# GpSimd's gathers wait, four by four, for marks that TensorE sets in its own program

## The chip, the cores and the metric

The kernel runs on one core of a Trainium2 chip. The metric is the device time of one execution in microseconds (us), the median of several runs. Engines are named as in the profile: PE is TensorE (PEld its weight loads), DVE is VectorE, ACT is ScalarE, POOL is GpSimd, SP is SyncE, whose DMA queue is SPq.

## The reference, cut to what matters

Thirty-two images of 64x64x3 go through a tokenizer of four spectral layers (a truncated Fourier transform, a product with weights for each mode, the transform back, a 1x1 convolution and a gelu). Its 64 tokens are put ahead of 128 text tokens, and the 192 tokens of each image go through four mixers: a recurrent one, a mixture of experts, an attention, and a product-key memory. The memory is the part that the change touches: each token and head picks 16 rows of a table of 32,768 rows, for the keys and the values alike, and sums them with softmax weights:

```python
kv_scores, indices = _pk(x, Wq_pk, pk_keys)           # 8 heads, 16 rows of 4096 each
ind = indices + offsets[None, None, :, None]
k = jnp.einsum('bnhk,bnhkd->bnhd', kv_scores, keys_table[ind])
v = jnp.einsum('bnhk,bnhkd->bnhd', kv_scores, values_table[ind])
sim = jnp.einsum('bihd,bjhd->bhij', q, k)             # causal softmax, then times v, then @ Wo
```

## The kernel before

The work is in pairs of images for the mixers (16 pairs, numbered 0 to 15) and in groups of four for the tokenizer (8 groups). A pair has 384 tokens, three tiles of 128. It needs 3 x 8 = 24 **units**, one per tile and head. A unit is 16 gathers: gather k fetches, for each of 128 tokens, the row of `in_table` (key and value side by side, 128 floats) that `IDX[:, tile, head, k]` names, into one of four slots of `GATH` (`RING = 4`, slot u % 4). So there are 384 gathers a pair and 6,144 in all, every one an indirect DMA that POOL issues at L670, and POOL does nothing else after its first memsets.

POOL's loop (`pool_gather`) walks the units in order. Ahead of units 0, 8 and 16 of a pair it waits until VectorE has written the indices of the tile (`kept_idx`), and ahead of each unit until VectorE has emptied the slot that unit u - 4 had (`gather_free`). Each unit then is used twice. ScalarE (`a_consume`, L886) waits for the 16 transfers and multiplies each with its weight, and VectorE (`v_consume`, L893) sums the 16 into `KV` and gives the slot back.

All other engines run a program whose order is fixed when it is built. A **round** works on three things side by side: the mixers of pair i + 1, up to the choice of its 16 rows a head; the gathered rows of pair i (chain "rows"), which ScalarE and VectorE take up; and the end of pair i - 1 (chain "back"); in the rounds that have it, also two layers of the next tokenizer group. `weave` lays chains beside each other in windows. Each chain has steps with costs in `STEPS`, a step comes up at the share of its chain's cost that lies ahead of it, and the step with the smallest share is next, on every engine in the same manner. A round has two large windows. In the first, the chain of rows is a step "hold" of cost 1 and then units 0 to 10 (`U1 = 11`); in the second it is units 11 to 23. So unit u of the first window stands at share (1 + u)/12. The first two rounds have their own lists (`first_rounds`): pair 0 has units 0 to 7 beside the first two tokenizer layers of group 1 ("alone"), then 8 to 15 and 16 to 23 in the two windows of "beside", beside the other two layers and the mixers of pair 1.

Each engine takes its instructions in order. Where ScalarE stands at a unit whose rows have not landed, all of its later work waits as well, and with it what TensorE needs from it. TensorE itself never touches the gathered rows; it first meets them as `KV`, in `t_back`.

`fence(e)` is one semaphore increment of the engine itself. It makes a semaphore instruction of its own, which carries a wait that stands ahead of it.

The gathers are issued in these lines of `pool_gather`:

```python
for u in range(NT3 * H):
    r = u % RING
    if u % H == 0: e.wait_ge(*event("kept_idx", i, u // H + 1))
    e.wait_ge(*event("gather_free", i, u + 1 - RING))
    fence(e)
    for k in range(TOPK):
        e.indirect_dma_start(GATH[:, r, k, :], None, table, bass.IndirectOffsetOnAxis(IDX[:, u // H, u % H, k:k + 1], 0)).then_inc(gath[r], 16)
```

Of the kernel before, what the change touches and what calls it, by code (L numbers as in the profile page):

```python
# [36 lines left out]
ROWQ = POS // 512  # L37
# [5 lines left out]
F_T = ROWQ + CHUNKS  # L43
# [37 lines left out]
NT3 = TOK // 128  # L81
E, FF, CAP = 8, 256, 960
H, TOPK, NK = 8, 16, 64
# [10 lines left out]
EPS = 1e-5  # L94
FMAX = float(np.finfo(np.float32).max)
RING = 4


FRONT = [("xT", 0, 1), ("rnn", 1, 2), ("rnn_back", 2, 1),
# [37 lines left out]
def total(plan, bank):  # L137
# [9 lines left out]
TOP_STEPS = 11  # L147

STEPS = {"coords": [2.2] * (GB * ROWQ), "forward0": [1.7] * F_T, "mix0": [5.3] * CHUNKS, "inverse0": [2.8] * CHUNKS + [2.2] * ROWQ,
         "tokens": [3.5] * (GB * ROWQ),  # L150
         "rnn": [4, 3, 2.5, 2.5, 1.2, 1.2, 1.2, 1.2], "moe": [2, 2.5, 2.5, 2.5, 3, 3, 3] + [4.6] * E + [6],
         "att": [2, 2.5, 2.5, 2.5, 1.5] + [3] * 5 + [3.3] * 6 + [5, 5], "pk": [2, 2.5, 2.5, 2.5, 1.5, 2.5, 2.5, 2.7, 2.7, 2.7],
         "top": [3, 3, 3, 3, 4, 4, 4, 4, 4, 4, 2] * NT3,
         "back": [3.5] * 3 + [2.6] * 4 + [2.2] * 3 + [7] * 7 + [4], "keep_x": [2], "rows": [1] * NT3 * H, "ahead": [1] * H, "hold": [1]}
STEPS.update({s + "1": STEPS[s + "0"] for s in ("forward", "mix", "inverse")})
BACK_IN = 3
U1 = 11
# [35 lines left out]
def whole(*sections):  # L193
    return [(s, 0, len(STEPS[s])) for s in sections]
# [5 lines left out]
def a_round(begin=(), layers=True, end=(), front=True, rows=True, back=True):  # L200


    tokenizer = [[*begin, *LAYER_0], ["forward1", "mix1", "inverse1", *end]] if layers else [[], []]
    turned = [("back", 0, BACK_IN)] if back else []
    return ([] if front else [[turned]]) + [
            [turned + whole("rnn", "moe", "att", "pk") if front else [], whole(*tokenizer[0]), whole("hold") + [("rows", 0, U1)] if rows else []],
            [whole("top") if front else [], [("back", BACK_IN, len(STEPS["back"]))] if back else [], whole(*tokenizer[1]),
             [("rows", U1, NT3 * H)] if rows else []],
            [whole("keep_x")]]


def first_rounds():


    alone = [[whole("rnn", "moe", "att", "pk")],
             [[("top", 0, TOP_STEPS)], whole("coords") + [("forward0", 0, ROWQ)]],
             [[("top", TOP_STEPS, len(STEPS["top"]))], [("forward0", ROWQ, F_T)] + whole(*LAYER_0[1:], *LAYER_1), whole("hold", "ahead")],
             [whole("keep_x")]]
    beside = [[whole("rnn", "moe", "att", "pk"), whole(*LAYER_0), [("rows", H, 2 * H)]],
              [whole("top"), whole(*LAYER_1, "tokens"), [("rows", 2 * H, NT3 * H)]],  # L220
              [whole("keep_x")]]
    return alone, beside

# [4 lines left out]
def early_fusion(nc, xT, fc0, sw, cwb, fc1, fc2, f1, f2, g3, g4, txt, wrnn, brnn, gw, w1, w2, b2, wq, wk, wv, wot, wpk, keysT, wq5, wo5,  # L228
# [3 lines left out]
    with ctx:  # L232
# [55 lines left out]
        empt = {(k, b): sem(f"{k}_out{b}") for k in PLANS for b in range(4)}  # L288
        PER = {"x_in": 80, "normed": 4, "shifted": 1, "exped": 1, "one_hot": 1, "h_kept": 1, "maxed": 24, "masked": 12,
               "rden": 2, "shift_top": NT3, "exp_top": NT3, "kept_idx": NT3, "kept_wt": NT3, "kept_x": 1,  # L290
               "gather_free": NT3 * H, "weighted": 1, "maxed5": 12, "scaled5": 6, "out_sb": 1, "stored": 16, "multiplied": NT3 * H}
        S = {n: sem(n) for n in PER}
        gath = [sem(f"gathered{r}") for r in range(RING)]
        tokenizer_in, const_in, zeroed = sem("tokenizer_weights_in"), sem("mixer_weights_in"), sem("buffers_zeroed"); mask_rows = sem("mask_rows_set")
# [6 lines left out]
        def fence(e):  # L301

            e.sem_inc(passed[str(e.engine).split(".")[-1]], 1)


        def event(name, it, k):

            return S[name], (it + 1) * PER[name] + k
# [352 lines left out]
        def pool_gather(e, i):  # L661
            for u in range(NT3 * H):
                r = u % RING

                if u % H == 0: e.wait_ge(*event("kept_idx", i, u // H + 1))

                e.wait_ge(*event("gather_free", i, u + 1 - RING))
                fence(e)
                for k in range(TOPK):
                    e.indirect_dma_start(GATH[:, r, k, :], None, table, bass.IndirectOffsetOnAxis(IDX[:, u // H, u % H, k:k + 1], 0)).then_inc(gath[r], 16)  # L670


# [416 lines left out]
        def q_slots(h, bank):  # L1089
# [2 lines left out]
            if h < 7: return [(QT[:, :, :, QSLOT[h], :], src)]  # L1092
            return [(QT[:, :, 2, 7, :], src[:, :, 0, :]), (QT[:, :, 0:2, 7, :], src[:, :, 1:3, :])]

        def t_turn(e, j, name, k):
            e.wait_ge(*event("normed", j, k))
            e.wait_ge(*free("front", j, name))
            fence(e)
            for t in range(NT3):
                m = e.transpose(PB[0][0:64, 128 * t:128 * t + 128], N[:, t, :], ID[:, :])  # L1100
            m.then_inc(full["front", 0], 1)
# [139 lines left out]
        def t_pk(e, j):  # L1241
            yield 4
            t_turn(e, j, "pkT", 4)
            yield 5
            e.wait_ge(*emptied("front", j, "pkT"))
            for n in range(4):
                yield 5 + n // 2
                name = ("qpkA", "qpkB")[n % 2]
                e.wait_ge(*free("front", j, name, n // 2))
                fence(e)  # L1250
                e.matmul(PB[2 + n % 2][:, 0:TOK], WPK[:, 128 * n:128 * n + 128], NT4[:, :], start=True, stop=True).then_inc(full["front", 2 + n % 2], 1)
            yield 7
            e.wait_ge(*emptied("front", j, "qpkA", 1)); e.wait_ge(*emptied("front", j, "qpkB", 1))
            for t in range(NT3):
                yield 7 + t
                for p in range(2):
                    name = ("simA", "simB")[p]
                    e.wait_ge(*free("front", j, name, t))
                    fence(e)
                    for hh in range(2):  # L1260
                        m = e.matmul(PB[2 + p][:, 256 * hh:256 * hh + 256], QPK[:, 2 * p + hh, 128 * t:128 * t + 128], KB[:, 2 * p + hh, :], start=True, stop=True)
                    m.then_inc(full["front", 2 + p], 1)
# [115 lines left out]
        def TENSOR(e, k, i, j, g, l):  # L1378
            return {"coords": lambda: t_coords(e, g), "forward0": lambda: t_forward(e, g, l, 0), "forward1": lambda: t_forward(e, g, l + 1, 0),
                    "mix0": lambda: t_mix(e, g, l), "mix1": lambda: t_mix(e, g, l + 1), "inverse0": lambda: t_inverse(e, g, l, 0), "inverse1": lambda: t_inverse(e, g, l + 1, 0),  # L1380
                    "tokens": lambda: t_tokens(e, g), "rnn": lambda: t_rnn(e, j), "moe": lambda: t_moe(e, j), "att": lambda: t_att(e, j),
                    "pk": lambda: t_pk(e, j), "back": lambda: t_back(e, k)}

        def SCALAR(e, k, i, j, g, l):
            return {"coords": lambda: a_coords(e, g), "forward0": lambda: a_forward(e, g, l, 0), "forward1": lambda: a_forward(e, g, l + 1, 0),
# [18 lines left out]
        @block.gpsimd  # L1404
        def _(e):
            def before(e):
                for t in (FW0, FW1, FW2, CONV, KB, ONES, RS, OHS, AREA4, SW, WO5):
                    e.memset(t[:], 1.0 if t is ONES else 0.0).then_inc(zeroed, 1)
            before(e)
            with e.Fori(0, PAIRS) as i:  # L1410
                pool_gather(e, i)

# [99 lines left out]
```

## Time and profile before

| what | us |
|---|---|
| median of 3 runs | 8628.49 |
| lowest and highest of them | 8618.34, 8636.04 |
| the profiled execution's own time | 8612.81 |
| its span in the trace | 8611.0 |
| POOL, first and last gather's start | 631.7, 8518.5 |
| POOL, sum of its gathers | 5933.5 |

The span is the part of the execution that the trace covers, 1.8 us less than the execution's own time. A busy time is the sum of an engine's instructions, without those that only wait, count or branch. For GpSimd a gather's busy time is the time in which it makes the descriptors, not the transfer. An idle time in brackets stands ahead of an instruction, with what ended it; "issue" there means that nothing the profile shows was waited for. L numbers are lines of the kernel before.

### The profile page before, as it was taken

How to read it: one execution, taken by the hardware profiler on the slowest of the kernel's cores; microseconds unless marked ns; L12 is line 12 of the kernel's file. 1: busy time of each engine (PE TensorE's matmuls, PEld its weight loads, DVE VectorE, ACT ScalarE, POOL GpSimd, SP SyncE). 2: the span in 40 equal slices, each digit the busy share in tenths (PEclk: the TensorE clock that was granted, in tenths of full speed). 3: DMA queues.
4: the chain of work that ended last, by engine and by line, in shares of the span. 5: the costliest groups of instructions: out<-in, count | busy, mean ns of one | idle time of the engine just before them, and what ended most of it. 6: DMA issues, size and time to landing. Idle time of an engine off the chain costs nothing.

```text
span 8611.0 us, 111801 instructions
## 1 busy us (share of the span) xinstructions
PE 6113.0 (71%) x30064; PEld 4613.3 (54%) x30064; DVE 4933.1 (57%) x16123; ACT 3291.5 (38%) x9885; POOL 5939.7 (69%) x6159
## 2 busy tenths in 40 slices
PE   6868979787877879787887879687887865242104
PEld 5547756666565646666565646566565643121103
DVE  1246484848575674847575674847566573736422
ACT  1213334444434344444443444344443443333222
POOL 0007667777777777777777777777777777777774
PEclk7766666666666666566656666566666665555555
DMA  1102222222222222222222222222222222121111
GB/s 30 17 7 68 52 52 59 60 59 60 63 60 61 60 57 61 60 60 60 63 60 60 60 58 61 58 62 60 63 60 58 59 58 53 51 54 51 53 53 32
DMA packets 660625, 471.63 MB, mean 55 GB/s; under 512 B 560624, under 2 KB 561008, under 8 KB 659632
## 3 DMA queue, kind: packets, MB, share of 16 engines
q0 software_dynamic: 196608, 403.05, 17.7%
q1 hardware_dynamic: 463344, 60.87, 4.5%
q8 instruction: 268, 4.39, 0.2%
q14 instruction: 405, 3.32, 0.1%
HBM read 461.32 MB, written 2.10 MB: 54 GB/s over the span
## 4 chain that ended last, share of the span: by engine, by line
POOL 60%; issue 20%; PE 13%; DVE 4%; SPq 1%; DVEq 1%; ACT 1%; DMA 1%; POOLq 0%; ACTq 0%
POOL GATH L670 60%; PE MM L457 3%; PE MM L472 1%; DVE KV L893 1%; PE PB L1205 1%; PE PB L1193 1%; PE MM L493 1%; PE MM L496 1%; PE MM L409 1%; PE TP L466 1%; PE PB L1141 1%; PE PB L1213 0%; PE PB L1172 0%; PE MM L432 0%; SPq L625 0%
## 5 line engine op out<-in xcount | busy, mean ns | idle before, releaser
L670 POOL DMA_INDIRECT GATH<-in_table,IDX x6144 | 5933.5, 966 | 2579.3 <-issue 2491.8
L886 ACT ACTIVATE GATH<-GATH,WT 128x128 f32<-128x128 f32 x6144 | 1883.3, 390 | 1961.1 <-DMA GATH<-in_table,IDX 1960.2
L893 DVE TENSOR_REDUCE KV<-GATH 128x128 f32<-128x2048 f32 x384 | 1392.8, 3627 | 1223.3 <-ACT GATH L886 1215.6
L457 PE MATMUL MM<-SPEC,SW 128*128 128x8 f32 (+1 forms) x8800 | 1153.5, 288 | 101.8 <-DMA SW<-in_sw 70.2
L457 PEld LDWEIGHTS MM<-SPEC,SW 128*128 128x128 f32 (+1 forms) x8800 | 1146.3, 248 | 139.4 <-issue 137.1
L566 DVE COPY TURN<-TP 80x512 f32<-80x512 f32 (+1 forms) x512 | 345.3, 684 | 451.1 <-PE TP L489 277.5
L1323 PE MATMUL PB<-AREA 128*64 128x64 f32 (+1 forms) x2304 | 317.5, 298 | 361.6 <-ACT AREA L1083 361.4
L409 PE MATMUL MM<-F,TURN 128*128 128x80 f32 x2048 | 367.2, 339 | 195.2 <-DVE TURN L566 191.3
L1323 PEld LDWEIGHTS PB<-AREA 128*64 128x64 f32 (+1 forms) x2304 | 255.3, 192 | 443.0 <-issue 395.0
L409 PEld LDWEIGHTS MM<-F,TURN 128*128 128x128 f32 x2048 | 337.8, 250 | 247.6 <-issue 186.8
L525 ACT ACTIVATE U<-MM 128x320 f32<-128x320 f32 (+1 forms) x416 | 218.7, 526 | 644.3 <-PE MM L409 390.9
L496 PEld LDWEIGHTS MM<-G,TURN 80*128 80x128 f32 x2048 | 315.0, 222 | 242.9 <-issue 125.2
L570 DVE COPY TURN<-TP 128x512 f32<-128x512 f32 (+1 forms) x320 | 216.9, 682 | 359.4 <-PE TP L466 212.2
L496 PE MATMUL MM<-G,TURN 80*128 80x128 f32 x2048 | 320.3, 307 | 69.0 <-DVE TURN L566 69.0
L493 PE MATMUL MM<-IMG,CONV 128*128 128x512 f32 x512 | 326.6, 725 | 29.0 <-ACT IMG L525 29.0
L472 PE MATMUL MM<-G,TURN 40*128 40x128 f32 x1280 | 300.4, 408 | 62.9 <-DVE TURN L570 62.7
L525 ACT ACTIVATE IMG<-MM,CONV 128x512 f32<-128x512 f32 x256 | 174.8, 684 | 434.8 <-PE MM L496 433.2
L472 PEld LDWEIGHTS MM<-G,TURN 40*128 40x128 f32 x1280 | 269.3, 304 | 111.1 <-issue 89.2
L1141 PE MATMUL PB<-NTR,W1E 104*128 104x384 f32 x512 | 279.6, 684 | 36.8 <-ACT AREA L984 36.8
L525 ACT ACTIVATE SPEC<-MM 128x160 f32<-128x160 f32 x320 | 95.1, 297 | 547.4 <-PE MM L457 308.0
L1205 PE MATMUL PB<-KT,AREA 64*128 64x192 f32 x768 | 260.2, 513 | 50.9 <-ACT AREA L1007 38.2
L869 DVE TENSOR_REDUCE PF<-SEARCH 128x16 f32<-128x800 f32 (+1 forms) x288 | 268.0, 931 | 30.7 <-issue 8.1
(214 smaller groups left out, 9843.0 us busy)
## 6 DMA issues: line engine op xcount, KB each, us to landing
GATH<-in_table,IDX POOLq DMA_INDIRECT x6144
SW<-in_sw SPq DMA_DIRECT2D x1280, 40.0 KB
CONV<-in_cwb SPq DMA_DIRECT2D x128, 4.0 KB
CONV<-in_cwb SPq DMA_DIRECT2D x128, 0.1 KB
U<-in_xT SPq DMA_DIRECT2D x16, 96.0 KB
out<-OUTB SPq DMA_DIRECT2D x16, 96.0 KB, 1.9
W1E<-in_w SPq DMA_DIRECT2D x1, 512.0 KB
W2E<-in_w SPq DMA_DIRECT2D x1, 512.0 KB
```

Source lines behind the costliest of these rows:

```text
L409: m = e.matmul(p[:, 80 * j:80 * j + 80], TURN[:, c % 2, 128 * j:128 * j + 128], F1[:, :], start=True, stop=True)
L457: m = e.matmul(pv[r, :, k, :], SW[r, half, k % HM, w:w + WID * beside], Sv[r, :, c * MODES + k, :], start=True, stop=True)
L472: m = e.matmul(p[:, 128 * a:128 * a + 128], TURN[0:40, i % 2, 128 * a:128 * a + 128], G3[:, :], start=True, stop=True)
L493: e.matmul(p[:, :], CONV[:, 0:128], IMG[:, q, 512 * c:512 * c + 512], start=True, stop=False, skip_group_check=True)
L496: m = e.matmul(p[:, 128 * j:128 * j + 128], TURN[0:80, (CHUNKS + c) % 2, 128 * j:128 * j + 128], G4[:, :], start=False, stop=True, skip_gr ...
L525: e.activation(dst, MM[n % 2][src] if not callable(src) else src(MM[n % 2]), func, **kw).then_inc(mm_out, 1)
L670: e.indirect_dma_start(GATH[:, r, k, :], None, table, bass.IndirectOffsetOnAxis(IDX[:, u // H, u % H, k:k + 1], 0)).then_inc(gath[r], 16)
L886: m = e.activation(GATH[:, r, k, :], GATH[:, r, k, :], ACT.Copy, scale=WT[:, u // H, u % H, k:k + 1])
L893: e.tensor_reduce(KV[:, u // H, :, u % H, :], GATH[:, u % RING, :, :].rearrange("p k (c d) -> p c d k", c=2), AX.X, ALU.add).then_inc(S["g ...
L1141: e.matmul(PB[2 + n % 2][:, 0:TOK], W1[:, 128 * n:128 * n + 128], NTR[:, :], start=True, stop=True).then_inc(full["front", 2 + n % 2], 1)
L1205: m = e.matmul(PB[2 + n % 2][:, SEQ * a:SEQ * a + SEQ], QT[:, b, r, 2 * c:2 * c + 2, :], KT[:, SEQ * b:SEQ * b + SEQ], start=True, stop=True)
L1323: m = e.matmul(o, PT[0:p0 + hi - lo, slot(c, p0), 64 * h:64 * h + 64], VW[0:p0 + hi - lo, t, h, :], start=(h == 0 and c == 0), stop=(h == ...
```

## The change

It adds a semaphore `paced` and a second counter of the work on it. TensorE gets a chain "pace" (and "pace_ahead" for the first third of pair 0) in the same windows as the chain of rows and with the same total cost: 96 steps a pair (`QUADS`), each of cost 4/16, each of which only adds 1 to the semaphore. Mark n of the first window thus stands at share (1 + n/4)/12 of it, where unit n/4 of the rows stands; marks 0 to 43 lie in the first window and 44 to 95 in the second. The chain stands in TensorE's list alone.

GpSimd gets, ahead of each four gathers (a **quad**, 96 a pair, quad n = 4u + k/4), a wait for the mark `LEAD = 8` quads behind it, and a fence: quad n may start once marks 0 to n - 8 of its pair are set. Quads 0 to 7 of a pair wait for the last marks of the pair before. The wait for the free slot and the one for the indices stay; the fence of each unit is gone, since the first quad's fence takes its place. GpSimd itself sets the first 96 counts, once, so that pair 0 starts with its first eight quads free.

```diff
--- before.py
+++ after.py
@@ -94,6 +94,9 @@
 EPS = 1e-5
 FMAX = float(np.finfo(np.float32).max)
 RING = 4
+QUAD = 4
+QUADS = 3 * 8 * 16 // QUAD
+LEAD = 8
 
 
 FRONT = [("xT", 0, 1), ("rnn", 1, 2), ("rnn_back", 2, 1),
@@ -151,7 +154,7 @@
          "rnn": [4, 3, 2.5, 2.5, 1.2, 1.2, 1.2, 1.2], "moe": [2, 2.5, 2.5, 2.5, 3, 3, 3] + [4.6] * E + [6],
          "att": [2, 2.5, 2.5, 2.5, 1.5] + [3] * 5 + [3.3] * 6 + [5, 5], "pk": [2, 2.5, 2.5, 2.5, 1.5, 2.5, 2.5, 2.7, 2.7, 2.7],
          "top": [3, 3, 3, 3, 4, 4, 4, 4, 4, 4, 2] * NT3,
-         "back": [3.5] * 3 + [2.6] * 4 + [2.2] * 3 + [7] * 7 + [4], "keep_x": [2], "rows": [1] * NT3 * H, "ahead": [1] * H, "hold": [1]}
+         "back": [3.5] * 3 + [2.6] * 4 + [2.2] * 3 + [7] * 7 + [4], "keep_x": [2], "rows": [1] * NT3 * H, "pace": [QUAD / 16] * QUADS, "pace_ahead": [QUAD / 16] * (QUADS // NT3), "ahead": [1] * H, "hold": [1]}
 STEPS.update({s + "1": STEPS[s + "0"] for s in ("forward", "mix", "inverse")})
 BACK_IN = 3
 U1 = 11
@@ -203,9 +206,9 @@
     tokenizer = [[*begin, *LAYER_0], ["forward1", "mix1", "inverse1", *end]] if layers else [[], []]
     turned = [("back", 0, BACK_IN)] if back else []
     return ([] if front else [[turned]]) + [
-            [turned + whole("rnn", "moe", "att", "pk") if front else [], whole(*tokenizer[0]), whole("hold") + [("rows", 0, U1)] if rows else []],
+            [turned + whole("rnn", "moe", "att", "pk") if front else [], whole(*tokenizer[0]), whole("hold") + [("rows", 0, U1)] if rows else [], whole("hold") + [("pace", 0, U1 * QUADS // 24)] if rows else []],
             [whole("top") if front else [], [("back", BACK_IN, len(STEPS["back"]))] if back else [], whole(*tokenizer[1]),
-             [("rows", U1, NT3 * H)] if rows else []],
+             [("rows", U1, NT3 * H)] if rows else [], [("pace", U1 * QUADS // 24, QUADS)] if rows else []],
             [whole("keep_x")]]
 
 
@@ -214,10 +217,10 @@
 
     alone = [[whole("rnn", "moe", "att", "pk")],
              [[("top", 0, TOP_STEPS)], whole("coords") + [("forward0", 0, ROWQ)]],
-             [[("top", TOP_STEPS, len(STEPS["top"]))], [("forward0", ROWQ, F_T)] + whole(*LAYER_0[1:], *LAYER_1), whole("hold", "ahead")],
+             [[("top", TOP_STEPS, len(STEPS["top"]))], [("forward0", ROWQ, F_T)] + whole(*LAYER_0[1:], *LAYER_1), whole("hold", "ahead"), whole("hold", "pace_ahead")],
              [whole("keep_x")]]
-    beside = [[whole("rnn", "moe", "att", "pk"), whole(*LAYER_0), [("rows", H, 2 * H)]],
-              [whole("top"), whole(*LAYER_1, "tokens"), [("rows", 2 * H, NT3 * H)]],
+    beside = [[whole("rnn", "moe", "att", "pk"), whole(*LAYER_0), [("rows", H, 2 * H)], [("pace", QUADS // 3, 2 * QUADS // 3)]],
+              [whole("top"), whole(*LAYER_1, "tokens"), [("rows", 2 * H, NT3 * H)], [("pace", 2 * QUADS // 3, QUADS)]],
               [whole("keep_x")]]
     return alone, beside
 
@@ -288,7 +291,7 @@
         empt = {(k, b): sem(f"{k}_out{b}") for k in PLANS for b in range(4)}
         PER = {"x_in": 80, "normed": 4, "shifted": 1, "exped": 1, "one_hot": 1, "h_kept": 1, "maxed": 24, "masked": 12,
                "rden": 2, "shift_top": NT3, "exp_top": NT3, "kept_idx": NT3, "kept_wt": NT3, "kept_x": 1,
-               "gather_free": NT3 * H, "weighted": 1, "maxed5": 12, "scaled5": 6, "out_sb": 1, "stored": 16, "multiplied": NT3 * H}
+               "gather_free": NT3 * H, "weighted": 1, "maxed5": 12, "scaled5": 6, "out_sb": 1, "stored": 16, "multiplied": NT3 * H, "paced": QUADS}
         S = {n: sem(n) for n in PER}
         gath = [sem(f"gathered{r}") for r in range(RING)]
         tokenizer_in, const_in, zeroed = sem("tokenizer_weights_in"), sem("mixer_weights_in"), sem("buffers_zeroed"); mask_rows = sem("mask_rows_set")
@@ -665,8 +668,10 @@
                 if u % H == 0: e.wait_ge(*event("kept_idx", i, u // H + 1))
 
                 e.wait_ge(*event("gather_free", i, u + 1 - RING))
-                fence(e)
                 for k in range(TOPK):
+                    if k % QUAD == 0:
+                        e.wait_ge(*event("paced", i, (TOPK * u + k) // QUAD + 1 - LEAD))
+                        fence(e)
                     e.indirect_dma_start(GATH[:, r, k, :], None, table, bass.IndirectOffsetOnAxis(IDX[:, u // H, u % H, k:k + 1], 0)).then_inc(gath[r], 16)
 
 
@@ -1092,6 +1097,11 @@
             if h < 7: return [(QT[:, :, :, QSLOT[h], :], src)]
             return [(QT[:, :, 2, 7, :], src[:, :, 0, :]), (QT[:, :, 0:2, 7, :], src[:, :, 1:3, :])]
 
+        def t_pace(e, i, lo, hi):
+            for n in range(lo, hi):
+                yield n
+                e.sem_inc(S["paced"], 1)
+
         def t_turn(e, j, name, k):
             e.wait_ge(*event("normed", j, k))
             e.wait_ge(*free("front", j, name))
@@ -1379,7 +1389,7 @@
             return {"coords": lambda: t_coords(e, g), "forward0": lambda: t_forward(e, g, l, 0), "forward1": lambda: t_forward(e, g, l + 1, 0),
                     "mix0": lambda: t_mix(e, g, l), "mix1": lambda: t_mix(e, g, l + 1), "inverse0": lambda: t_inverse(e, g, l, 0), "inverse1": lambda: t_inverse(e, g, l + 1, 0),
                     "tokens": lambda: t_tokens(e, g), "rnn": lambda: t_rnn(e, j), "moe": lambda: t_moe(e, j), "att": lambda: t_att(e, j),
-                    "pk": lambda: t_pk(e, j), "back": lambda: t_back(e, k)}
+                    "pk": lambda: t_pk(e, j), "pace": lambda: t_pace(e, i, QUADS // NT3 if isinstance(i, int) and i == 0 else 0, QUADS), "pace_ahead": lambda: t_pace(e, j, 0, QUADS // NT3), "back": lambda: t_back(e, k)}
 
         def SCALAR(e, k, i, j, g, l):
             return {"coords": lambda: a_coords(e, g), "forward0": lambda: a_forward(e, g, l, 0), "forward1": lambda: a_forward(e, g, l + 1, 0),
@@ -1407,6 +1417,7 @@
                 for t in (FW0, FW1, FW2, CONV, KB, ONES, RS, OHS, AREA4, SW, WO5):
                     e.memset(t[:], 1.0 if t is ONES else 0.0).then_inc(zeroed, 1)
             before(e)
+            e.sem_inc(S["paced"], PER["paced"])
             with e.Fori(0, PAIRS) as i:
                 pool_gather(e, i)
```

GpSimd's program changes as follows. These are the rows at the start of its loop over pairs, before, for units 0 and 1 (`kept_idx` and `gather_free` are the waits):

```order
L667 ISA [waits kept_idx]
L670 DMA GATH<-in_table,IDX 128x128 [waits gather_free]
L670 DMA GATH<-in_table,IDX 128x128 x15
L667 REGISTER_ALU
L670 DMA GATH<-in_table,IDX 128x128 [waits gather_free]
L670 DMA GATH<-in_table,IDX 128x128 x15
```

And the end of unit 0 and the start of unit 1 after the change:

```order
L675 DMA GATH<-in_table,IDX 128x128 [waits paced]
L675 DMA GATH<-in_table,IDX 128x128 x3
L673 REGISTER_ALU
L675 DMA GATH<-in_table,IDX 128x128 [waits paced]
L675 DMA GATH<-in_table,IDX 128x128 x3
L670 REGISTER_ALU
L673 REGISTER_ALU [waits gather_free]
L675 DMA GATH<-in_table,IDX 128x128 [waits paced]
```

Every fourth gather now has a register instruction and a wait ahead of it, where before only every sixteenth had. The gathers and their order are the same.

On TensorE no matrix instruction moves. These are the rows of the rounds' loop near the end of the first window of an odd pair, before:

```order
L493 MATMUL MM<-IMG,CONV 128x512
L494 REGISTER_ALU
L496 MATMUL MM<-G,TURN 128x128 x4
L489 MATMUL TP<-IDB,U 80x128 x4
L493 MATMUL MM<-IMG,CONV 128x512
```

And after:

```order
L496 MATMUL MM<-IMG,CONV 128x512
L497 REGISTER_ALU
L499 MATMUL MM<-G,TURN 128x128 x4
L492 MATMUL TP<-IDB,U 80x128 x4
L496 MATMUL MM<-IMG,CONV 128x512
```

The list leaves out instructions that only count, so the marks are not seen in it: mark 36 of the odd pairs is set between the third and the fourth row (L499 and L492 after, L496 and L489 before).

## Rows read from the trace of the kernel before

**Rows 1.** The page, part 1 and part 2: busy time and span in slices.

```profile
PE 6113.0 (71%) x30064; PEld 4613.3 (54%) x30064; DVE 4933.1 (57%) x16123; ACT 3291.5 (38%) x9885; POOL 5939.7 (69%) x6159
...
POOL 0007667777777777777777777777777777777774
```

**Rows 2.** The page, part 4: chain that ended last.

```profile
POOL 60%; issue 20%; PE 13%; DVE 4%; SPq 1%; DVEq 1%; ACT 1%; DMA 1%; POOLq 0%; ACTq 0%
```

**Rows 3.** The page, part 5: gathers, their weighting, their sum (mean ns after busy us).

```profile
L670 POOL DMA_INDIRECT GATH<-in_table,IDX x6144 | 5933.5, 966 | 2579.3 <-issue 2491.8
L886 ACT ACTIVATE GATH<-GATH,WT 128x128 f32<-128x128 f32 x6144 | 1883.3, 390 | 1961.1 <-DMA GATH<-in_table,IDX 1960.2
L893 DVE TENSOR_REDUCE KV<-GATH 128x128 f32<-128x2048 f32 x384 | 1392.8, 3627 | 1223.3 <-ACT GATH L886 1215.6
```

**Rows 4.** Line L670: ns least, middle, most; first and last start.

```profile
L670 POOL DMA_INDIRECT GATH<-in_table,IDX x6144: 938/944/2368, 631.7 to 8518.5; - x199
```

**Rows 5.** Waits, 3158 to 3645 us (pair 5): us in total, times, longest.

```profile
POOL GATH L670 <- issue: 117.0, 384, 0.3
ACT GATH L886 <- DMA GATH<-in_table,IDX: 65.9, 9, 12.0
```

**Rows 6.** Waits, 631 to 1175 us (pair 0).

```profile
POOL GATH L670 <- DVE KV L893: 55.4, 8, 19.8
```

**Rows 7.** Waits, 1175 to 1693 us (pair 1).

```profile
POOL GATH L670 <- DVE KV L893: 32.0, 11, 12.5
```

**Rows 8.** Line L893 around 1030 us, and in time order GpSimd's next gather.

```profile
L893 DVE TENSOR_REDUCE KV<-GATH x1: 3644/3644/3644, 1032.0 to 1032.0; 128x128 f32<-128x2048 f32 x1
...
1036.45 0.94 POOL L670 DMA_INDIRECT GATH<-in_table,IDX  x1 [19.80 <-DVE KV L893]
```

**Rows 9.** Time order, GpSimd: first gather of unit 11, pairs 1, 3, 5, 7, 11.

```profile
1419.35 1.35 POOL L670 DMA_INDIRECT GATH<-in_table,IDX  x1 [0.30 <-issue]
...
2404.09 1.46 POOL L670 DMA_INDIRECT GATH<-in_table,IDX  x1 [0.30 <-issue]
...
3378.03 0.94 POOL L670 DMA_INDIRECT GATH<-in_table,IDX  x1 [0.30 <-issue]
...
4352.94 0.95 POOL L670 DMA_INDIRECT GATH<-in_table,IDX  x1 [0.30 <-issue]
...
6304.46 1.03 POOL L670 DMA_INDIRECT GATH<-in_table,IDX  x1 [0.30 <-issue]
```

**Rows 10.** Time order, TensorE: what follows mark 36, same five pairs.

```profile
1455.97 0.85 PE L489 MATMUL TP<-IDB,U 128*80 128x128 f32 x3
...
2403.14 0.60 PE L489 MATMUL TP<-IDB,U 128*80 128x128 f32 x4
...
3385.07 0.85 PE L489 MATMUL TP<-IDB,U 128*80 128x128 f32 x3
...
4354.01 0.63 PE L489 MATMUL TP<-IDB,U 128*80 128x128 f32 x2
...
6306.90 0.63 PE L489 MATMUL TP<-IDB,U 128*80 128x128 f32 x2
```

**Rows 11.** Time order, GpSimd: two waits of pair 1.

```profile
1440.65 0.94 POOL L670 DMA_INDIRECT GATH<-in_table,IDX  x1 [1.02 <-DVE KV L893]
...
1465.63 0.94 POOL L670 DMA_INDIRECT GATH<-in_table,IDX  x1 [5.32 <-DVE KV L893]
```

**Rows 12.** Time order, around 1338 and 1368 us: unit 6 of pair 1, gathered and taken up.

```profile
1338.21 0.94 POOL L670 DMA_INDIRECT GATH<-in_table,IDX  x1 [0.30 <-issue]
...
1367.96 1.26 ACT L886 ACTIVATE GATH<-GATH,WT 128x128 f32<-128x128 f32 x4
```

**Rows 13.** Time order, 2980 to 2985 us: long gathers beside VectorE.

```profile
2981.59 0.99 DVE L863 TENSOR_TENSOR SEARCH<-IOTA,PF 128x800 f32<-128x800 f32 x1
...
2981.76 1.64 POOL L670 DMA_INDIRECT GATH<-in_table,IDX  x1 [0.30 <-issue]
...
2982.66 0.99 DVE L866 TENSOR_TENSOR SEARCH<-SEARCH 128x800 f32<-128x800 f32 x1
```

## The prediction

> **What bounds the kernel now.** I read the busy times first, and they mislead: TensorE is busy for 6113.0 us and GpSimd for 5939.7 us, and neither reaches 72% of the span [rows 1]. The chain that ended last decides: 60% of it lies on GpSimd and 20% is "issue" [rows 2]. The gathers explain both numbers. There are 6144 of them, and of the 2579.3 us of idle time ahead of them 2491.8 us are "issue" [rows 3]. In pair 5 all 384 gathers have such an idle time, 117.0 us in all and at most 0.3 us each [rows 5], so a gather costs 0.944 us (the middle one) and a gap of 0.305 us, a cadence of 1.25 us. From the first gather at 631.7 us to the last at 8518.5 us [rows 4] lie 7887 us; 6143 cadences are 7673 us. The rest is 134 us by which gathers are longer than 0.944 us (5933.5 less 6144 x 0.944) [rows 3] and waits for VectorE, 55.4 us in pair 0 and 32.0 us in pair 1 [rows 6, 7]. So GpSimd issues without a pause from pair 2 on, and all others wait for it: ScalarE's weighting stands idle for 1960.2 us until gathers land [rows 3]. Only pairs 0 and 1 are bound by the other engines. Whatever stops GpSimd lengthens the kernel, unless it replaces a stop that is there already.
>
> **What the change does to this.** It removes and speeds up nothing on GpSimd. It adds a condition: a gather may run at most two units (8 quads) ahead of TensorE's place, where the ring lets it run four units ahead of VectorE's sums. I laid the 1,536 marks into TensorE's own order of matrix instructions, read when the instruction behind each mark started, and compared that with the start of the quad that would wait for it. The terms follow from this and from the added instructions.
>
> **Pairs 0 and 1.** Here TensorE is behind the gathers: by that count about three quarters of the marks come after the start of their quad, up to 53 us in pair 0. As the other engines set the pace here, what counts is the last mark that binds. That is mark 36 of pair 1, needed by the first gather of unit 11. The gather started at 1419.35 us [rows 9], and TensorE passed the mark just before 1455.97 us [rows 10]. A stopped gather also needs time to start again: VectorE's sum that frees a slot ended at 1032.0 + 3.644 = 1035.64 us and the gather began at 1036.45 us, 0.8 us later [rows 8]. So the unit starts at 1456.8 us, 37.4 us later. Behind it the kernel before had two stops, 1.02 and 5.32 us, each with the normal 0.3 us in it [rows 11]; a later GpSimd does not meet them: 37.4 - 0.7 - 5.0 = **31.7 us**. Then the others are late too. The last gather of unit 6 of pair 1 started at 1338.21 us, so it ended at 1339.15 us, and ScalarE took the unit up at 1367.96 us, 28.8 us later [rows 12]. By my pass over the marks GpSimd is some 33 us late there, and ScalarE takes rows up 2 us after the last gather where it waits, so it begins 33 + 2 - 28.8 = **6 us** late, and the marks behind with it. Together 38 us. In plain words: the lead of the ring, four units against two, is what GpSimd lived on while the others caught up, and about two units' time (2 x 20 us) is lost once.
>
> **Pairs 2 to 12.** All is in step with GpSimd, so a delay of GpSimd moves the marks as well, and the margins of the trace hold. The tight place is again mark 36, near the end of the first window. In the even pairs it is set 4 us or more in time. In the odd ones, with 0.8 us for the restart: pair 3, 2403.14 + 0.8 against 2404.09, just in time; pair 5, 3385.07 + 0.8 - 3378.03 = 7.8 us late; pair 7, 4354.01 + 0.8 - 4352.94 = 1.9 us; pair 9 has the same margin as pair 7; pair 11, 6306.90 + 0.8 - 6304.46 = 3.2 us [rows 9, 10]. Sum **15 us**. Pairs 13 to 15 have no tokenizer beside them and are 7 us or more in time: 0.
>
> **TensorE's own marks.** No row shows what one costs. The nearest: ahead of a unit's first gather GpSimd runs two small instructions, ahead of units 8 and 16 three, and all hide in a gap of 0.3 us [rows 5], so one is at most 0.1 us. Forty-four marks lie ahead of the tight place: 0 to 4.4 us in each of the six odd pairs up to 11, 0 to 26 us. Most fall where TensorE waits or has matrix work queued; I take 1 us each, **6 us**. Elsewhere they cost nothing while TensorE idles, which is its cover.
>
> **GpSimd's own instructions.** The new boundaries carry one register instruction and one wait, just what unit starts carried, and those 24 of pair 5 show no longer gap than the other 360 [rows 5]: 0. Only ahead of units 0, 8 and 16 there is one more than any boundary had: 48 x 0 to 0.1 = 0 to 5 us; I take **0**, since the gap has held every smaller number. Behind the waiting instruction stand all later gathers, and behind these ScalarE's weighting, VectorE's sum and through them TensorE; that is why nothing of the stops is hidden in pairs 2 to 12. The head up to 631.7 us and the tail behind the last gather are not touched; the one count that GpSimd sets at the start falls in the head.
>
> The Trainium skill ("Advanced Engine Details and Errata", Miscellaneous Facts) gives 50 to 100 ns for a sequencer's reading of a semaphore. Taken as time added to each of the 1,536 new waits that would be 77 to 154 us, an estimate from that page, and the sum would be 136 to 213 us. The trace's unit starts speak against it.
>
> **Sum:** 31.7 + 6 + 15 + 6 + 0 = 59 us. The profiled execution took 8612.8 us, so its like would take 8672 us; the median of the runs is 15.7 us above it, so I forecast 8628.5 + 59 = **8687 us**. Its own range is 8655 (only 32 in pairs 0 and 1 and a few us after them) to 8725 (marks at their upper bound, 20 us more, and pairs as tight as pair 5 more often). A measurement of this kernel can tell 0.2%, 17 us, from no change.
>
> **Rivals.**
> *No change that can be measured.* GpSimd stops 87.4 us in pairs 0 and 1 already [rows 6, 7]; if the marks' stops only take their place, and the others, with fewer gathers in flight, catch up sooner, 0 to 17 us remain: 8629 to 8645 us. It also holds the case that the marks never bind. Against it: the margins of rows 9 and 10 are 37 us in pair 1, and only 5.7 us of stops come behind it to be replaced. Chance 0.12.
> *Each wait has a price.* If the quads' boundaries aren't covered as the unit starts are, 1,536 waits at 0.05 to 0.1 us (the upper bound above and half of it) add 77 to 154 us: 8764 to 8841 us. It decides as soon as a plain boundary's gap is above 0.31 us. Chance 0.10.
> *Late everywhere.* The margins of pairs 1 to 11 are small against what TensorE's marks and its clock can move. If mark 36 comes 6 us later in all of them, even pairs begin to stop as well: about 11 x 6 = 66 us more, 8753 us. Chance 0.10.
> *Faster.* VectorE's search for the top rows lengthens gathers: the one at 2981.76 us took 1.64 us, while L863 and L866 ran beside it [rows 13]; all such excess is 134 us. If the pacing moved gathers off this work, up to 134 us come back: 8687 - 134 = 8553 us. It decides where more than 76 of the 134 us go. Against it: GpSimd still issues without a pause, so gathers can't be moved off anything; what it stops is 1% of its time. Chance 0.05.
> The Trainium skill ("GPSIMD Engine Reference", Specifications) says that GpSimd shares its SBUF interfaces with VectorE and contends with instructions that have two SBUF inputs; by that rule only gathers that don't meet L863 and L866 gain, and the trace agrees with its 1.64 against 0.94 us.
>
> **How the numbers follow.** The forecast has 0.63, and the rivals in their order 0.12, 0.10, 0.10 and 0.05. A range from 8637 to 8790 us leaves out the faster case, half of the no-change case, two thirds of the priced waits and the outer edges of the forecast, and keeps the late marks: about 8 in 10. Faster by over 0.2%: 0.05; within: 0.12; slower: 0.83.
>
> **What would show it.** Right: gathers of pairs 0 and 1 idle for some 110 us in all with TensorE's marks as what ended it, the last gather of pair 1 about 38 us later, pairs 2, 4, 6 with no stop, odd pairs with one of 2 to 8 us near unit 11, plain gaps still 0.30 us. The steps fail if the gap at quad boundaries is longer, if even pairs stop, or if the start of pair 2 has not moved.

## The result and the profile after

The change makes the kernel slower: 8660.70 us median (8646.95 to 8668.83, 8 runs) against 8633.45 us (8618.34 to 8640.72, 8 runs), a ratio of 1.0033 with a 95% interval of 1.0024 to 1.0042, or 21 to 36 us. The profiled execution took 8646.95 us with a span of 8645.1 us, 34 us more than that of before.

The page of the changed kernel: busy times, GpSimd's slices, the chain that ended last, and the three groups that handle the gathered rows (busy us, mean ns; idle us ahead of them and what ended most of it). They answer to [rows 1 to 3].

```profile
PE 6084.4 (70%) x30064; PEld 4590.2 (53%) x30064; DVE 4934.1 (57%) x16123; ACT 3291.4 (38%) x9885; POOL 5960.8 (69%) x6159
...
POOL 0007667777777777777777777777777777777774
...
POOL 36%; PE 30%; issue 15%; DVE 10%; ACT 3%; DMA 2%; PEld 2%; DVEq 1%; SPq 1%; POOLq 1%; PEldq 0%; ACTq 0%
...
L675 POOL DMA_INDIRECT GATH<-in_table,IDX x6144 | 5954.6, 969 | 2592.8 <-issue 2448.4
L891 ACT ACTIVATE GATH<-GATH,WT 128x128 f32<-128x128 f32 x6144 | 1883.5, 390 | 2101.4 <-DMA GATH<-in_table,IDX 2100.6
L898 DVE TENSOR_REDUCE KV<-GATH 128x128 f32<-128x2048 f32 x384 | 1392.4, 3626 | 1272.5 <-ACT GATH L891 1266.4
```

The busy times are those of before within 0.5%. The chain that ended last looks different, since it now crosses over to TensorE in the stops, and even where GpSimd never stops it may be followed back through the marks; it names TensorE for 30% of the span although nothing of TensorE got slower. The idle time ahead of the gathers tells more. Idle beyond the plain gap of 0.305 us, which I call **stops** from here on, is 2592.8 - 625.8 (ahead of the first gather) - 6143 x 0.3048 = 94.6 us; for the kernel before the same sum is 2579.3 - 624.9 - 1872.4 = 82.0 us [rows 3]. The rest of the 34 us is not idle time: the gathers themselves took 5954.6 us, 21.1 us more than before.

Line L675, the least, middle and longest gather in ns, and the starts of the first and last:

```profile
L675 POOL DMA_INDIRECT GATH<-in_table,IDX x6144: 939/947/2363, 632.5 to 8553.3; - x199
```

Between these starts lie 7920.8 us, before 7886.9 us [rows 4]. The middle gather took 947 ns and not 944; the experiments bear on whether that is the change's doing.

Where the stops are: waits of GpSimd in pair 0 (632 to 1200 us), then of GpSimd and ScalarE in pair 1 (1200 to 1716 us), then GpSimd's longest idle time behind it (total us, times, longest). These answer to [rows 5 to 7].

```profile
POOL GATH L675 <- PEq L1103: 77.9, 33, 12.6
...
ACT GATH L891 <- DMA GATH<-in_table,IDX: 84.7, 8, 14.5
...
POOL GATH L675 <- PEq L1103: 27.8, 22, 15.7
...
POOL GATH L675 <- issue: 1600.5, 5250, 0.3
```

"PEq L1103" is TensorE's sequencer at the line of the marks. A wait that doesn't stop anything still counts its 0.3 us. Pairs 0 and 1 have all the stops; from pair 2 on the longest idle time is 0.3 us at the 5,250 gathers of that row, and the others, put down to marks (120) or sums (7), have 0.3 us each as well. The waits for VectorE's sums (55.4 and 32.0 us before [rows 6, 7]) are gone, TensorE's marks stand in their place, and ScalarE, which waited for landing rows at units 21 and 23 of pair 1 before (6.5 and 5.5 us), now waits at unit 6 and at each from 16 on: 84.7 us up to unit 22 and 11.1 us at unit 23.

In time order, ScalarE in pair 1 of the changed kernel, at units 6 and 16:

```profile
1365.92 1.28 ACT L891 ACTIVATE GATH<-GATH,WT 128x128 f32<-128x128 f32 x4 [1.03 <-DMA GATH<-in_table,IDX]
...
1572.76 2.45 ACT L891 ACTIVATE GATH<-GATH,WT 128x128 f32<-128x128 f32 x8 [13.40 <-DMA GATH<-in_table,IDX]
```

And at unit 16 in the kernel before (the row begins with the last of unit 15):

```profile
1560.87 2.44 ACT L886 ACTIVATE GATH<-GATH,WT 128x128 f32<-128x128 f32 x8
```

Unit 6 is taken up at 1365.92 us, which is 2 us sooner than before [rows 12], though its last gather came 25 us later (1363.4 against 1338.2). Unit 16 is taken up 11 us later, after ScalarE stood idle for 13.40 us. So in this execution ScalarE's own timetable up to unit 15 of pair 1 hardly changed; it ran out of gathered rows for good at unit 16 and not at unit 21. Pair 2 begins at 1716.3 us and not at 1693.8, and this 22.5 us stays to the end.

### The profile page after: what moved, and what is told of

The parts are those of the page before. It is cut to its first block, busy times and chain, and to the rows that moved or that the text cites. A ratio compares the mean times of both kernels' runs of the same rounds, so it can differ in the third digit from the quotient of the medians.

```text
span 8645.1 us, 116003 instructions
## 1 busy us (share of the span) xinstructions
PE 6084.4 (70%) x30064; PEld 4590.2 (53%) x30064; DVE 4934.1 (57%) x16123; ACT 3291.4 (38%) x9885; POOL 5960.8 (69%) x6159
## 4 chain that ended last, share of the span: by engine, by line
POOL 36%; PE 30%; issue 15%; DVE 10%; ACT 3%; DMA 2%; PEld 2%; DVEq 1%; SPq 1%; POOLq 1%; PEldq 0%; ACTq 0%
POOL GATH L675 36%; PE MM L460 5%; DVE KV L898 2%; PE PB L1151 2%; PE PB L1203 2%; PE PB L1215 2%; PE PB L1223 2%; PE PB L1182 2%; ACT GATH L891 2%; PE MM L475 2%; DMA GATH<-in_table,IDX 1%; PE MM L496 1%; PE MM L393 1%; PE MM L499 1%; PE MM L412 1%
## 5 line engine op out<-in xcount | busy, mean ns | idle before, releaser
L675 POOL DMA_INDIRECT GATH<-in_table,IDX x6144 | 5954.6, 969 | 2592.8 <-issue 2448.4
L499 PEld LDWEIGHTS MM<-G,TURN 80*128 80x128 f32 x2048 | 316.7, 223 | 234.0 <-issue 126.8
L499 PE MATMUL MM<-G,TURN 80*128 80x128 f32 x2048 | 321.6, 308 | 62.4 <-DVE TURN L569 62.3
L496 PE MATMUL MM<-IMG,CONV 128*128 128x512 f32 x512 | 324.7, 721 | 38.7 <-ACT IMG L528 38.7
```

What stands on the lines that cost most here:

```text
L496: e.matmul(p[:, :], CONV[:, 0:128], IMG[:, q, 512 * c:512 * c + 512], start=True, stop=False, skip_group_check=True)
L499: m = e.matmul(p[:, 128 * j:128 * j + 128], TURN[0:80, (CHUNKS + c) % 2, 128 * j:128 * j + 128], G4[:, :], start=False, stop=True, skip_gr ...
```

## The experiments

Each ratio compares a kernel with the kernel before on the same chip. The last three columns come from one profiled execution each. Stops are computed as above from the page's row. "First to last" is from the start of the first gather to the start of the last. One chip ran the change a second time, the waits that never bind and the two kernels with waits in a part of the pairs; another ran the two leads and the ring. Which one ran the first comparison, with the profiles of the first two rows, isn't known. So the three columns can also differ by the chip; the ratios can't.

| kernel | ratio, 95% interval | stops, us | gathers, us | first to last, us |
|---|---|---|---|---|
| before | 1 | 82.0 | 5933.5 | 7886.9 |
| the change | 1.0033, 1.0024 to 1.0042 | 94.6 | 5954.6 | 7920.8 |
| the change, second time | 1.0041, 1.0027 to 1.0054 | 120.3 | 5941.3 | 7933.1 |
| waits that never bind | 1.0005, 0.9996 to 1.0014 | 84.5 | 5945.4 | 7901.4 |
| waits in pairs 0, 1 | 1.0031, 1.0020 to 1.0041 | 114.9 | 5938.0 | 7924.4 |
| waits from pair 2 | 1.0009, 1.0000 to 1.0018 | 87.9 | 5937.6 | 7896.9 |
| lead of 12 quads | 1.0012, 1.0003 to 1.0021 | 92.5 | 5936.4 | 7900.4 |
| lead of 6 quads | 1.0137, 1.0119 to 1.0154 | 212.4 | 5933.5 | 8017.3 |
| ring of three, no marks | 1.0029, 1.0017 to 1.0041 | 105.7 | 5934.1 | 7911.2 |

### The change a second time

No edit.

> The change itself once more, for a second trace. Of its first profiled execution's 34 us, 12 us are stops of GpSimd (94.4 us against 82.3, all in pairs 0 and 1), 21 us are gathers that take longer (5954.6 us against 5933.5), 1 us is the start. Theory A (the lead is lost once, gathers vary by chance from one execution to the next): again 25 to 30 us in the median; stops 90 to 98 us in pairs 0 and 1 and none behind them; the gathers' sum lands anywhere between 5930 and 5960 us. Theory B (the gathers are longer because of the change): their sum is again 5950 us or more, the common gather 947 ns, not 944.

Measured: 1.0041, 1.0027 to 1.0054. The gathers' row of its page, then GpSimd's waits behind pair 1 (1724 to 8564 us), then, in time order, the first gather of unit 11 of pair 3 and the matrix instruction behind mark 36:

```profile
L675 POOL DMA_INDIRECT GATH<-in_table,IDX x6144 | 5941.3, 967 | 2616.5 <-issue 2438.3
...
POOL GATH L675 <- issue: 1590.2, 5213, 1.5
...
POOL GATH L675 <- PEq L1103: 58.5, 156, 3.6
...
2434.49 0.94 POOL L675 DMA_INDIRECT GATH<-in_table,IDX  x1 [2.50 <-PEq L1103]
...
2438.39 0.42 PE L492 MATMUL TP<-IDB,U 128*80 128x128 f32 x1
```

The stops in pairs 0 and 1 are larger than in the first profile (108 us), and here some lie behind them too: 58.5 us of waits less 156 x 0.305 us of plain gaps are 11 us of the 12 us of stops there, at units 11 to 13 of pairs 3, 5 and 9. Both differ from what was expected (90 to 98 us, and none). The gathers' sum lies between the two others, with a middle of 945 ns. The last two rows show something that I had read wrongly: the gather that mark 36 released began 3.9 us before the matrix instruction that stands behind the mark. TensorE's sequencer sets a mark when it comes to it, while earlier matrix work is still running.

### All waits there, none that binds

```diff
-LEAD = 8
+LEAD = 64
```

> LEAD = 64 in place of 8: every mark, wait and fence is there, but no wait for a mark can stop GpSimd, since the ring stops it first. Theory A: ratio 1.000, within 0.1%; stops are back to about 82 us, for VectorE's sums. Theory B: 10 to 20 us slower than before, gathers' sum 5950 us or more. The rival of the prediction in which each of the 1,536 waits has a price: 77 us or more.

Measured: 1.0005, 0.9996 to 1.0014. The page's row of the gathers, GpSimd's waits in pairs 0 and 1 (633 to 1704 us), and behind them:

```profile
L675 POOL DMA_INDIRECT GATH<-in_table,IDX x6144 | 5945.4, 968 | 2583.8 <-issue 2463.4
...
POOL GATH L675 <- DVE KV L898: 61.8, 16, 13.7
...
POOL GATH L675 <- PEq L1103: 30.8, 17, 19.9
...
POOL GATH L675 <- issue: 1610.4, 5285, 0.3
```

The longest idle time behind pair 1 is 0.3 us at 5,285 gathers, the plain gap. The marks on TensorE and the 1,536 waits and fences on GpSimd cost -3 to 12 us together, nothing that can be told from zero. The rival in which each wait has a price of 77 us or more falls. The stops are back at 84.5 us, near the 82.0 us of the kernel before. (The profile still names TensorE for a part of them, since it infers releasers; a wait for a mark 64 quads back can't have ended them, the ring must.) The gathers took 12 us longer than in the profile of before, which stays under theory B's sum of 5950 us, and the ratio's interval holds only the low end of theory B's 10 to 20 us.

### Waits in pairs 0 and 1 alone, and from pair 2 on alone

The loop of GpSimd's first two pairs is unrolled in both, and only the flag differs:

```diff
-        def pool_gather(e, i):
+        def pool_gather(e, i, paced):
...
-                    if k % QUAD == 0:
+                    if paced and k % QUAD == 0:
                         e.wait_ge(*event("paced", i, (TOPK * u + k) // QUAD + 1 - LEAD))
                         fence(e)
+                    if not paced and k == 0: fence(e)
...
-            with e.Fori(0, PAIRS) as i:
-                pool_gather(e, i)
+            for i in range(2): pool_gather(e, i, True)
+            with e.Fori(2, PAIRS) as i:
+                pool_gather(e, i, False)
```

In the second kernel True and False change places.

> The waits for marks stand in pairs 0 and 1 alone (their loop is unrolled; pairs 2 to 15 wait as before the change). Theory A: as slow as the change, 25 to 30 us. Theory B: about half of that, 12 to 18 us, since 7/8 of the quads' waits are gone; the common gather 944 ns again.

> The converse: pairs 0 and 1 as before the change, waits for marks from pair 2 on. Theory A: ratio 1.000, within 0.1%, with no stop behind pair 1, or one of a few us where an odd pair is as tight as the trace of before made it look (mark 36, unit 11). Theory B: 10 to 20 us slower, all of it in longer gathers. The prediction's term for pairs 2 to 12 would be 15 us of stops here.

Measured: 1.0031 (1.0020 to 1.0041) for pairs 0 and 1 alone. The gathers' row, GpSimd's waits for TensorE up to the start of pair 2 (630 to 1731 us), and its idle time behind it:

```profile
L676 POOL DMA_INDIRECT GATH<-in_table,IDX x6144 | 5938.0, 966 | 2611.3 <-issue 1894.9
...
POOL GATH L676 <- PEq L1104: 90.3, 44, 10.9
...
POOL GATH L676 <- issue: 1636.8, 5371, 0.3
```

It is as slow as the change, with 7/8 of the waits gone and the common gather at 944 ns. Theory B had 12 to 18 us (1.0014 to 1.0021) for it, which the interval just touches; theory A's 25 to 30 us lie in its middle. In this profile some stops in pairs 0 and 1 are put down to "issue", so the 90.3 us are not all of them; by the row of the gathers there are 114.9 us.

Measured: 1.0009 (1.0000 to 1.0018) for the converse. The gathers' row, and GpSimd's waits from pair 2 on (1693.5 to 8531 us):

```profile
L676 POOL DMA_INDIRECT GATH<-in_table,IDX x6144 | 5937.6, 966 | 2586.8 <-issue 1835.8
...
POOL GATH L676 <- issue: 1594.9, 5228, 1.5
...
POOL GATH L676 <- PEq L1104: 52.6, 144, 3.6
```

Here 52.6 us less 144 x 0.305 are 9 us of true stops (10 us with those put down to "issue"), at units 11 to 13 of pairs 3, 7, 9 and 11. So the tight place of the odd pairs is real, and it costs 0 to 16 us by the ratio; the gathers took 5937.6 us although all of the waits from pair 2 on are in. This kernel's first two pairs are unrolled as in the other one, so the unrolling costs no more than these 16 us either.

### The lead as a dose

```diff
-LEAD = 8
+LEAD = 12
```

> LEAD = 12: GpSimd may run three units ahead of TensorE's place in place of two. Theory A (what is lost is lead, once, in pairs 0 and 1): about 12 us slower than before, between never_binds (none) and the change (27), no stop behind pair 1. The rival that any binding wait for a mark costs its restart of 0.9 us, however large the lead: as slow as the change.

Measured: 1.0012, 1.0003 to 1.0021, or 3 to 18 us. The gathers' row and the idle time behind pair 1:

```profile
L675 POOL DMA_INDIRECT GATH<-in_table,IDX x6144 | 5936.4, 966 | 2592.6 <-issue 2457.0
...
POOL GATH L675 <- issue: 1608.9, 5279, 0.3
```

That is what theory A had (about 12 us, no stop behind pair 1). The rival in which any binding wait costs its restart, however large the lead, falls: it would be as slow as the change, and the two intervals (up to 1.0021, from 1.0024) don't meet.

```diff
-LEAD = 8
+LEAD = 6
```

> LEAD = 6: one and a half units of lead. Theory A with the margins of the trace: 45 to 70 us are lost in pairs 0 and 1, and then nearly every pair stops, since the tight place near the end of the first window has 3 to 7 us of margin at LEAD = 8 and a cadence of 10 us is taken from it; sum about 195 us, 100 to 250. If the steady rounds follow GpSimd without limit (the consumers simply come earlier), only 45 to 70 us.

Measured: 1.0137, 1.0119 to 1.0154, or 103 to 133 us. The gathers' row, GpSimd's waits for TensorE in pairs 0 and 1 (631 to 1740 us), and behind them:

```profile
L675 POOL DMA_INDIRECT GATH<-in_table,IDX x6144 | 5933.5, 966 | 2709.2 <-issue 2417.0
...
POOL GATH L675 <- PEq L1103: 134.0, 55, 15.1
...
POOL GATH L675 <- issue: 1569.3, 5134, 1.3
...
POOL GATH L675 <- PEq L1103: 157.2, 240, 7.7
```

Behind pair 1 there are 157.2 - 240 x 0.305 = 84 us of stops put down to marks (89 us with those put down to "issue"). Every pair up to 14 has one at unit 10, near the end of the first window, 5.2 us in most odd ones and 3.6 us in most even ones; the odd pairs up to 11 have more of 2 to 3 us, at unit 1 and from pair 7 on at unit 12. In pairs 0 and 1 the stops are 124 us, 42 more than before, a little under the 45 to 70 expected. The sum is in the expected range but below its 195 us: my pass overstated how far the stops of the steady rounds add up.

### The other wait made shorter: a ring of three

```diff
-RING = 4
+RING = 3
```

This edits the kernel before; it has no marks.

> The kernel before with three slots of GATH in place of four, no marks at all. It takes a unit of lead away by the other wait, the one for VectorE's sum. Theory A: 15 to 25 us slower, all in pairs 0 and 1, as GpSimd comes to the end of pair 1 a unit (20 us) later; behind it single stops of at most 2 us, as the free slot is at hand 19 to 50 us early with four. The rival that the loss belongs to the marks (TensorE's semaphore traffic, GpSimd's extra waits): within 0.1% of before.

Measured: 1.0029, 1.0017 to 1.0041, or 15 to 35 us. The gathers' row, GpSimd's waits for VectorE in pairs 0 and 1 (636 to 1725 us), and its idle time behind them:

```profile
L670 POOL DMA_INDIRECT GATH<-in_table,IDX x6144 | 5934.1, 966 | 2607.5 <-issue 2492.7
...
POOL GATH L670 <- DVE KV L893: 108.6, 25, 21.1
...
POOL GATH L670 <- issue: 1632.3, 5356, 0.3
```

With no mark, no added wait and the gathers as short as before (5934.1 us), one unit less of lead costs what the change costs. The stops are 23.7 us more than before, all of them ahead of pair 2.

## Why the prediction was right, and where its sizes were off

The forecast was 59 us over before and 8687 us, the measured 27.3 us and 8660.7 us, within the forecast's own range (8655 to 8725) near its lower end. The direction and the mechanism hold; two terms were too large. That the time fell into the range is in part luck: the lower end, 8655, stands 26.5 us over the 8628.5, less than the "32 in pairs 0 and 1 and a few us after them" that explain it, and the kernel before measured 8633.45 us in the comparison, 5 us above the forecast's base. The 27.3 us lie below the explained lower end of some 35 us.

**The signs it named.** GpSimd's idle times put down to marks in pairs 0 and 1 are 77.9 + 27.8 = 105.7 us (110 forecast), pairs 2, 4 and 6 have no stop, and the plain gap is 0.30 us. The start of pair 2 moved, by less than 38 us in both profiles of the change. The stops near unit 11 of odd pairs are missing in the first profile and are there in the second, in pairs 3, 5 and 9. Part of the first rival came true as well: the marks' stops did take the place of VectorE's 82 us, so that the sum of stops rose by only 13 us in the first profile and by 38 us in the second.

**What bounds the kernel** held. From pair 2 on GpSimd has nothing but plain gaps, before and after, and head and tail didn't move: the last gather starts 92 us before the end in both. So the time changes by what changes between the first and the last gather: longer stops or longer gathers.

**Pairs 0 and 1: 38 us forecast.** The start of pair 2, counted from the first gather, is 1062.1 us before, 1070.3 with waits that never bind and 1060.3 with waits from pair 2 on, 1064 in the mean. With the binding waits in pairs 0 and 1 it is 1083.8, 1093.8 and 1100.4, in the mean 1093: 28 us, with one execution up to 17 us from another. Of the 28 us some 24 are stops and 4 are longer gathers. The step that was off first is "TensorE passed the mark just before 1455.97 us". I took the start of the matrix instruction behind a mark as its time. In both profiles of the change the record of mark 36 of pair 1 lies 2.6 us before that start, and elsewhere up to 4.8 us. In time order, the first gather of unit 11 of pairs 1 and 5 of the changed kernel, and then the matrix instruction behind mark 36 of both:

```profile
1446.83 0.95 POOL L675 DMA_INDIRECT GATH<-in_table,IDX  x1 [0.30 <-issue]
...
3403.24 0.94 POOL L675 DMA_INDIRECT GATH<-in_table,IDX  x1 [0.30 <-issue]
...
1448.34 0.38 PE L492 MATMUL TP<-IDB,U 128*80 128x128 f32 x2
...
3400.52 0.38 PE L492 MATMUL TP<-IDB,U 128*80 128x128 f32 x2
```

The gather of pair 1 started 1.5 us before its matrix instruction, not 0.8 us behind it, and the instruction itself came at 1448.34 us and not at 1455.97; so the unit was 27.5 us late (1446.83 against 1419.35 [rows 9]) and not 37.4. Nor did mark 36 stop it: its idle time is the plain 0.30 us, in both profiles of the change. The marks before it did. The largest stop of pair 1 is at unit 2 (quad 8, which needs mark 0), and the last ahead of unit 11 is at unit 10 (quad 43, which needs mark 35). In time order, in the first profile:

```profile
1261.55 0.94 POOL L675 DMA_INDIRECT GATH<-in_table,IDX  x1 [15.75 <-PEq L1103]
...
1441.83 0.95 POOL L675 DMA_INDIRECT GATH<-in_table,IDX  x1 [1.42 <-PEq L1103]
```

With the waits in pairs 0 and 1 alone, mark 36 did stop unit 11, for 2.3 us. The forecast named the right stretch, and its one mark stood at the edge of binding. In the second profile the same matrix instruction came at 1456.5 us, so the other engines' timetable moves by several us from one execution to the next, and by which step the 8 us came isn't shown. The second addend, 6 us because ScalarE "begins late, and the marks behind with it", was not seen as a cause: at unit 6 ScalarE waited 1.03 us for rows and still was 2 us sooner than before. In the second profile it took the unit up at 1373.68 us, 5.7 us later than before, but waited only 0.88 us for it; it had been 6.3 us late already at unit 0 (1273.91 against 1267.63 us), where it didn't wait for rows.

**Pairs 2 to 12: 15 us forecast.** Measured 0 us in the first profile of the change, 11 in the second, 9 with the waits from pair 2 on. The place is the right one (units 11 to 13 of odd pairs), and again the 2.6 us were missing: by them pair 5 would have been 5 us late, and pairs 7, 9 and 11 at most 1 us. With a lead of 6 the same place, a unit earlier, stops every pair from 2 to 14, which shows how small the margin is. "Pairs 13 to 15 are 7 us or more in time" doesn't follow from the rule used for the others: in the trace of before the matrix instruction behind mark 36 of pair 13 starts at 7282.57 us, 1.25 us after its gather (7281.32). The one ahead of the mark starts at 7272.29 us. There was no stop in pair 13, so here too the instruction behind is the wrong place to read. The rival of late marks everywhere (8753 us) falls: no even pair stopped with a lead of 8.

**TensorE's marks and GpSimd's waits: 6 and 0 us forecast.** Waits that never bind cost -3 to 12 us with both in. The plain gap ahead of a quad with a wait is still 0.305 us. The 50 to 100 ns a reading that the Trainium skill ("Advanced Engine Details and Errata", Miscellaneous Facts) gives do not add up here: the estimated 77 to 154 us would have been a ratio of 1.009 to 1.018. How long a reading took no row shows; it fits into a gap that is there anyway.

**The faster rival.** The gathers did not become shorter. Over nine executions their sum lies between 5933.5 and 5954.6 us: 5933.5 and 5934.1 without marks, 5933.5 to 5954.6 with them. The first profile of the change is 34 us longer and not 13 because its gathers are. That the highest values fell on the change itself and on the waits that never bind looked like an effect of the change. The kernels with leads of 12 and 6, which have all the same instructions, have 5936.4 and 5933.5 us, but on a chip where the ring of three, which has none of them, has 5934.1 us; on the chip of the second time the four sums are 5937.6 to 5945.4 us. So execution, chip and change aren't told apart here, and what sets the common length to 944, 945 or 947 ns stays open. The medians bound it: all marks and waits together cost at most 12 us when none binds, and the loss came in full with 7/8 of the waits gone. Nor did the pacing move gathers off VectorE's work: 1,287 gathers of the kernel before overlap a TENSOR_TENSOR of VectorE and 1,301 after.

**The mechanism in one sentence**, as the runs show it: in pair 0 the other engines need more than the 20 us in which GpSimd gathers a unit (ScalarE took up units 0 to 23 from 656.1 to 1220.2 us in the trace of before, 24.5 us a unit), GpSimd fills the ring and lives off it when they catch up (units 0 to 21 of pair 1 from 1267.6 to 1652.0 us, 18.3 us a unit), and whatever caps its lead, mark or ring, makes the point where all wait for GpSimd come earlier. The dose follows: a lead of 64 quads, 12, 8 and 6 adds about 0.5 (not told from zero), 1.2, 3.3 to 4.1 and 13.7 thousandths. A larger ring is what the experiments point to as an improvement, by no more than the 82 us of stops that are there. It wasn't tried: the ring has to divide the 24 units, and two more slots are 16 KB a partition, which this kernel's other buffers don't leave.

## What to carry to other kernels

Where one engine's queue sets the time and runs without a pause, as GpSimd's did here, a pacing wait in it takes nothing off that queue; in these runs it only cost. Ask what the lead that it cuts is used for: here it paid for a start-up phase, so the loss came once, until the cap met the tightest place of the steady rounds and came in every round. To forecast such a wait, lay the new signals into the old trace and compare place by place, but read a signal's time at the sequencer, some us ahead of the matrix instruction behind it, and take one execution's timetable as uncertain by several us.

## What the runs showed of the hardware

A semaphore wait and a register instruction between two indirect DMAs of GpSimd cost nothing that can be seen when the wait is satisfied: 0.305 us from one gather's end to the next one's start with and without them, at up to 96 places a pair. A wait that does stop GpSimd is followed by its gather 0.86 us after TensorE's mark, in both profiles of the change the smallest distance of any mark and its quad; less the plain gap, half a microsecond of a stop is thus the restart. TensorE's sequencer runs ahead of its matrix instructions: in the median of all 1,536 marks even the instruction ahead of the mark started 2.4 us after the mark's record, in both profiles of the change, and it started after the record at 97% of them. Gathers are lengthened by VectorE's TENSOR_TENSOR instructions beside them: in the kernel before, the 1,287 gathers that overlap one are together 132.7 us longer than the middle gather, the 4,857 others 0.8 us. And the same gather has a common length of 944, 945 or 947 ns in different executions, worth up to 18 us over 6,144 of them, two thirds of this change's effect, from a cause that stays open.
